# A gated cross-attention and expert layer on one core: result rows in 4 KB pieces, reloads on two queues, a short block moved up, and four sums shared by two engines

## The reference

```
x = x + tanh(g0) * attention(layernorm(x), ctx)      # one head; keys: 64 of ctx and 64 of x per sequence
x = x + tanh(g1) * moe(layernorm(x))
moe(xf):
  probs = softmax(xf @ gate_w.T)                      # 8 experts
  top_p, top_i = top_k(probs, 2)
  y  = sum over the 2 experts of top_p * (silu(xf @ fc1_e.T) * (xf @ fc2_e.T)) @ proj_e.T     # width 176
  y += sigmoid(xf @ shared_gate.T) * (silu(xf @ s1.T) * (xf @ s2.T)) @ shared_proj.T          # width 704
```

## Time and profile before

| | |
|---|---|
| median of 3 executions | 301.57 us (300.46 to 302.14) |
| profiled execution | 300.09 us, span 298.3 us |
| TensorE busy | 276.1 us (93%) |
| VectorE busy | 215.4 us (72%) |
| ScalarE busy | 170.5 us (57%) |
| GpSimd busy | 131.5 us (44%) |
| last chain, largest | TensorE 55%, VectorE 24%, ScalarE 8% |

### The profile page before, as it was taken

How to read it: one execution, slowest core, us unless ns; L and a number is a source line. 1 busy time by engine, 2 the same in 40 slices (tenths; PEclk the granted TensorE clock), 3 DMA queues, 4 the chain that set the end, 5 groups by cost and what they waited for, 6 DMA issues and landing times.

```text
span 298.3 us, 5868 instructions
## 1 busy us (share of the span) xinstructions
PE 276.1 (93%) x1785; PEld 247.7 (83%) x1785; DVE 215.4 (72%) x698; ACT 170.5 (57%) x399; POOL 131.5 (44%) x163
## 2 busy tenths in 40 slices
PE   3987999999998899999999999799999999999991
PEld 3876878789787687798888888699999999998881
DVE  3864876979968858767876767877877787763285
ACT  1666777688557447574235465366676667654230
POOL 3430541451685245445550000057777787775000
PEclk9999999999999999999999999999999999999998
DMA  7470216212027021544324654358888888756796
GB/s 209 167 248 4 73 55 230 70 53 73 20 65 280 21 91 55 192 142 139 129 77 163 218 196 143 103 107 141 130 141 138 137 135 142 117 68 71 258 355 233
DMA packets 30511, 40.18 MB, mean 135 GB/s; under 512 B 2961, under 2 KB 26641, under 8 KB 30481
## 3 DMA queue, kind: packets, MB, share of 16 engines
q1 hardware_dynamic: 22336, 29.53, 31.5%
q0 software_dynamic: 7152, 9.57, 19.4%
q10 hardware_dynamic: 992, 0.71, 0.8%
HBM read 22.68 MB, written 17.11 MB: 133 GB/s over the span
## 4 chain that ended last, share of the span: by engine, by line
PE 55%; DVE 24%; ACT 8%; issue 6%; POOL 3%; DMA 3%; DVEq 0%; SPq 0%; ACTq 0%; POOLq 0%
PE bank L415 42%; PE bank L658 6%; DVE ew_lo L1011 4%; PE bank L753 3%; ACT ew_hi L776 3%; DVE work L1341 3%; PE bank L709 3%; ACT sh_hi L776 2%; DVE neg_max L1055 2%; DVE xt_lo L1011 2%; DVE work L1363 2%; ACT work L808 1%; DMA xn_all<-x_dram 1%; DVE sh_lo L1011 1%; DMA weight_stage<-ew_dram 1%
## 5 line engine op out<-in xcount | busy, mean ns | idle before, releaser
L1533 POOL DMA_INDIRECT y_d<-work,dest_of_slot x39 | 60.5, 1552 | 56.9 <-DVE dest_of_slot L1387 55.3
L415 PE MATMUL bank<-ew_hi,xt_hi 128*128 (+2 forms) x172 | 53.7, 322 | 1.1 <-DVE xt_lo L1011 0.8
L415 PE MATMUL bank<-ew_lo,xt_hi 128*128 (+2 forms) x172 | 51.8, 301 | 0.0
L415 PE MATMUL bank<-ew_hi,xt_lo 128*128 (+1 forms) x133 | 40.5, 305 | 0.0
L1011 DVE TENSOR_TENSOR xt_lo<-bank,xt_hi 128x256 fp32r<-128x256 f32 (+2 forms) x90 | 35.6, 398 | 3.0 <-ACT xt_hi L776 1.5
L1493 POOL DMA_INDIRECT xs_d<-xn_all,slot_of_pair x32 | 32.9, 1029 | 10.1 <-issue 7.3
L415 PE MATMUL bank<-xt_hi,sw_hi 128*128 128x512 f32 x88 | 34.8, 395 | 0.2 <-DVE work L1341 0.2
L776 ACT ACTIVATE xt_hi<-bank 128x256 fp32r<-128x256 f32 (+1 forms) x90 | 32.7, 409 | 3.4 <-PE bank L753 2.2
L415 PE MATMUL bank<-xt_lo,sw_hi 128*128 128x512 f32 x88 | 34.5, 392 | 0.0
L415 PE MATMUL bank<-xt_hi,sw_lo 128*128 128x512 f32 x88 | 34.3, 390 | 0.0
L1011 DVE TENSOR_TENSOR ew_lo<-bank,ew_hi 128x512 fp32r<-128x512 f32 (+1 forms) x41 | 22.7, 581 | 15.9 <-ACT ew_hi L776 15.7
(11 more groups left out here) (159 smaller groups left out, 680.9 us busy)
## 6 DMA issues: line engine op xcount, KB each, us to landing
work<-xs_d SPq DMA_DIRECT2D x39, 136.0 KB, 2.5
weight_stage<-ew_dram SPq DMA_DIRECT2D x10, 486.5 KB, 3.8
ew_hi<-y_d SPq DMA_DIRECT2D x8, 512.0 KB, 7.6
y_d<-work SPq DMA_DIRECT2D x6, 512.0 KB, 3.7
work<-ctx_t_dram SPq DMA_DIRECT2D x4, 512.0 KB, 3.7
xn_all<-x_dram SPq DMA_DIRECT2D x3, 512.0 KB, 6.0
xs_d<-pad_row SPq DMA_DIRECT2D x9, 136.0 KB, 1.8
weight_stage<-sw_dram SPq DMA_DIRECT2D x3, 384.0 KB, 3.4
```

Source lines behind the costliest of these rows:

```text
L415: last = nc.tensor.matmul(dst, a, b, start=(n == 0), stop=(n == len(pairs) - 1))
L1533: nc.gpsimd.indirect_dma_start(out=y2_d, out_offset=bass.IndirectOffsetOnAxis(ap=IX[:, n:n + 1], axis=0), in_=EY[:, n % 4, :], in_offset=None,
```

## The change

There are five edits.

- A token's row in `y2_d` is now `(chunk, p, j)` and no longer `(chunk, j, p)`, so the four rows of a partition are adjacent and one piece of a store or reload is 4 KB where it was 1 KB. `C_TOK` follows.
- The reloads of copy 1 are issued by ScalarE, two behind `s_hi(3,1)` (after its own wait for all scatters) and two behind `s_hi(3,2)`; SP issues those of copy 0.
- In the last chunk TensorE's order becomes `... pj(3,2), fc(3,4), fc(3,5), pj(3,3), pj(3,4), pj(3,5)`.
- Combines 4 and 5 stand between product and low half of blocks 4 and 5, one each; they stood behind the low half of block 4, both. Combines 6 and 7 stay behind the low half of block 5.
- The four sums of chunk 2 are split. VectorE does tile 0 ahead of the expert steps (waiting for that tile alone, `p_pre`) and tile 1 at the end of step 0; ScalarE does tiles 2 and 3 at the end of step 0 (`a_z`). TensorE's steps 1, 2 and 3 wait for the bank that each needs. `v_z` counts two less from there.

```
-        y2_t = y2_d[0:TOP * N_TOK, :].rearrange("(i c j p) d -> i c p j d", i=TOP, c=N_CH, j=TPC)
+        y2_t = y2_d[0:TOP * N_TOK, :].rearrange("(i c p j) d -> i c p j d", i=TOP, c=N_CH, j=TPC)
...
             def store_sums(s):
-                sp.wait_ge(v_z, 4 * s + 4)
+                sp.wait_ge(v_z, 4 * s + 4 if s < PRE - 1 else 4 * s + 2)
+                if s == PRE - 1:
+                    sp.wait_ge(a_z, 2)
...
             for c in LAST_FIRST:
-                for i in range(TOP):
-                    sp.dma_start(Y2[i][:, c * TPC:(c + 1) * TPC, :], y2_t[i, c]).then_inc(d_y[i][c], 16)
+                sp.dma_start(Y2[0][:, c * TPC:(c + 1) * TPC, :], y2_t[0, c]).then_inc(d_y[0][c], 16)
...
+                    if (s, j) == (PRE - 1, S_FULL) and t < TPC - 1:
+                        last.then_inc(p_pre, 1)
...
-                if s == 1:
-                    pe.wait_ge(v_z, 4 * PRE)
+                if s in (1, 2):
+                    pe.wait_ge(v_z, 4 * (PRE - 1) + s)
+                if s in (2, 3):
+                    pe.wait_ge(a_z, s - 1)
...
-            blocks(PRE, N_CH, 1)
+            fc(LAST, 1)
+            for j in range(2, S_BLK):
+                if j < S_FULL:
+                    pj(LAST, j - 2)
+                fc(LAST, j)
+            for j in range(S_FULL - 2, S_BLK):
+                pj(LAST, j)
...
+                if s == 0:
+                    act.wait_ge(d_z, 16 * (PRE - 1))
+                    for t in (2, 3):
+                        T = (PRE - 1) * TPC + t
+                        if t == 2:
+                            act.wait_ge(p_pre, 3)
+                        else:
+                            act.wait_ge(p_pj, 6 * PRE)
+                        copy(SX2[:, t, :], B[4 + t][:, 0:D], scale=GS[:, T:T + 1]).then_inc(a_z, 1)
...
+            for j in range(S_BLK):
+                s_silu(LAST, j)
+                s_hi(LAST, j)
+                if j == 1:
+                    for r in range(4):
+                        act.wait_ge(d_ey[r], 16 * len(range(r, SLOT_TILES, 4)))
+                if j in (1, 2):
+                    for c in LAST_FIRST[2 * j - 2:2 * j]:
+                        act.dma_start(Y2[1][:, c * TPC:(c + 1) * TPC, :], y2_t[1, c]).then_inc(d_y[1][c], 16)
...
+                if s == 0:
+                    dve.wait_ge(p_pre, 2)
+                    s_sum(PRE - 1, 1)
...
-            s_sums(PRE - 1)
+            dve.wait_ge(d_z, 16 * (PRE - 1))
+            dve.wait_ge(p_pre, 1)
+            s_sum(PRE - 1, 0)
             e_steps(e_step)
 
             for j in range(S_BLK):
                 s_mult(LAST, j)
-                if j == 3:
-                    combine(0)
+                if j >= 3:
+                    combine((0, 4, 5)[j - 3])
                 s_lo(LAST, j)
...
-                if j == 4:
-                    combine(4)
-                    combine(5)
-                if j == 5:
-                    combine(6)
-                    combine(7)
-            s_sums(LAST)
+            combine(6)
+            combine(7)
+            for t in range(TPC):
+                s_last(t)
...
-    consts[:, C_TOK:C_DUM] = np.arange(TOP * N_T)[None, :] * P + np.arange(P)[:, None]
+    tile = np.arange(TOP * N_T)
+    consts[:, C_TOK:C_DUM] = (tile // TPC * CH + tile % TPC)[None, :] + np.arange(P)[:, None] * TPC
```

More of the change, by code:

```diff
@@ L227, in build @@
         g_pay, e_ix = map(sem, ("g_payload", "e_ix"))
+        p_pre, a_z = sem("p_pre"), sem("a_z")
         zeroed, tanh_g, rw_hi, rw_lo = map(sem, ("zeroed", "tanh_g", "rw_hi", "rw_lo"))
@@ L401, in _ @@
             for t in range(LAST * TPC + 1, N_T, 2):
-                sp.wait_ge(v_z, t + 1)
+                sp.wait_ge(v_z, t - 1)
                 sp.dma_start(out_t[t], XNR[:, t, :]).then_inc(d_out, 16)
@@ L655, in pj @@
                             pe.wait_ge(v_hl, 6 * s + j + 1)
-                        if j == 0 and n == 0 and s > 0:
+                        if j == 0 and n == 0 and 0 < s < LAST:
                             pe.wait_ge(v_z, 4 * s - 3 + t)
@@ L680, in _, with blocks @@
             pe.wait_ge(sw_lo, SW_PIECES)
-            def blocks(s0, s1, ahead):
-                order = [(s, j) for s in range(s0, s1) for j in range(S_BLK)]
+            def blocks(ahead):
+                order = [(s, j) for s in range(PRE) for j in range(S_BLK)]
                 for n in range(ahead, len(order) + 2):
-                    if n == len(order) and s1 == PRE:
+                    if n == len(order):
                         pe.wait_ge(v_h, 6 * PRE - 1)
@@ L689, in blocks @@
                         xx(1, 1, 16)
-                    if n == len(order) + 1 and s1 == PRE:
+                    if n == len(order) + 1:
                         pe.wait_ge(ew_lo, E_PIECES)
@@ L766, in _ @@
             pj(0, 1)
-            blocks(0, PRE, 4)
+            blocks(4)
             e_steps(e_step)
             pe.wait_ge(e_h, SLOT_TILES)
-            blocks(PRE, N_CH, 1)
+            fc(LAST, 1)
[5 more added lines that the diff above has]
+                pj(LAST, j)
         @block.scalar
@@ L1002, in _ @@
             for t in range(LAST * TPC, N_T, 2):
-                act.wait_ge(v_z, t + 1)
+                act.wait_ge(v_z, t - 1)
                 act.dma_start(out_t[t], XNR[:, t, :]).then_inc(d_out, 16)
@@ L1352, in expert_weights, with s_sum, s_last @@
                     .then_inc(ew_lo, 1)
+            def s_sum(s, t):
+                T = s * TPC + t
+                nc.vector.tensor_scalar(SX2[:, t, :], B[4 + t][:, 0:D], GS[:, T:T + 1], None, ALU.mult).then_inc(v_z, 1)
             def s_sums(s):
[L1355 to L1358, removed]
-                    dve.wait_ge(v_c2, 2)
[L1360 to L1367, removed]
+                dve.wait_ge(p_pj, 6 * s + 6)
+                at_least(dve, d_z, 16 * s)
+                for t in range(TPC):
+                    s_sum(s, t)
+            def s_last(t):
+                T = LAST * TPC + t
+                if t == 0:
+                    dve.wait_ge(v_c2, 2)
+                dve.wait_ge(p_end, t + 1)
+                nc.vector.scalar_tensor_tensor(out=XNR[:, T, :], in0=B[4 + t][:, 0:D], scalar=GS[:, T:T + 1],
+                                               in1=XNR[:, T, :], op0=ALU.mult, op1=ALU.add).then_inc(v_z, 1)
             def e_step(s, u, m):
```

## The result

Twenty executions of each kernel: 299.91 us after (298.49 to 302.04), 301.88 before. The ratio is 0.9933, interval 0.9915 to 0.9950, which is 2.0 us of 301.88. The forecast was 298.8, 2.8 less than before; the measured time lies in its range of 297.7 to 300.4. The direction was right, and 0.8 us of gain didn't come. So the two spans must not be subtracted: the joints are compared by distances inside one trace.

What follows compares the result with a forecast made beforehand. TensorE, busy throughout the expert steps, was taken as the bound, so only that stretch's two ends pay: 300.09 - 1.6 (start) - 1.3 (tail) + 0.1 (stores) = 297.3, plus 1.48 is 298.8 us; range 297.7 to 300.4.

Steps and rivals of the forecast that it cites:

- Start: Entry to the expert steps: splitting chunk 2's sums lets up(3) start earlier; gain taken as 1.6 us, lower bound 0.95.
- The 0.35 "issue" gap: TensorE ahead of up(2): register work behind a blocked queue, 0.35 us, taken as gone; up to two such gaps possible.
- Rival C: Expert-step start pays half: ScalarE's copies and VectorE's sum delay step 1, or register gaps stay; gain 0.6, 299.8; chance 0.11.
- the signs named for the right case: Trace checks, among them TensorE idle under 0.3 us between up(1) and up(2), and up(3) 5.8 us after up(0).
- Tail: Last chunk after fc(3,4): new block order and combine places start the last sums earlier; gain 1.33 us, bounds 0.5 to 1.4.
- T: End of fc(3,4) on TensorE, 286.72 us in the profile before; the forecast's tail times count from it.
- the landing of the third pair: Chunk 1's reloads: landed at 287.3 in the old profile; margin ahead of combine 4 of 0.7 us, 1.6 at 396 GB/s.
- rival B: Tail: a combine waits for its reload, holding up VectorE and pj(3,4); 2.0 us late gives 300.1; chance 0.11.
- Second queue: Reloads: engines are full with one queue at a DMA share of 1.09, so a second was priced at nothing.
- the 0.1 for the stores: Last stores at the kernel's end: 0.1 us added to the sum for the last 1.57 MB going out.
- rival D: Expert steps: scatters slow down with the new row order; landing 7.5 us costs 6.7 us, 306; chance 0.05.
- rival E: Both joints: no effect at all, since they wait for something the trace puts elsewhere; 301.5; chance 0.06.

Runs made afterwards that it cites:

- the register experiment: Changed kernel with up(3)'s registers and addresses made ready in step 2 ahead of pj(0)'s wait, and up(3) issued ahead of pj(1)'s address work; ratio 0.9909.
- combines early: Changed kernel with each combine moved one place earlier in the last chunk, 5 beside block 4, 6 beside block 5, 7 last; ratio 0.9929.

## Why the prediction was right, and where it missed

**Start.** Forecast 1.6, measured 1.02 (8.43 to 7.41). The mechanism was right in every step that was named: the sum alone takes 0.48 (0.47 forecast), the product is through in time for the transposes behind up(1), ScalarE's two copies delay its silu by 0.03 only (3.46 after up(0), 3.43 before), and pj(0) doesn't wait. The term that was mis-sized is "The 0.35 "issue" gap ... I take it as gone". It moved from up(2) to up(3) and grew to 0.41, and restarting a chain cost another 0.23 (1.20 for six matmuls instead of 0.97): 0.64, which the register experiment gave back as 0.65. The lower bound, 0.95, covered it. The measured 1.02 was shown to be this edit's own by the kernel with the sums only (1.04); since the old start varies from 8.43 to 8.83 and the new one from 7.33 to 7.56, one pair of traces fixes it to a few tenths only. Rival C, "the start pays half", came true in part: its second cause, the register gaps, held, its first didn't, and the gain lies between its 0.6 and the forecast's 1.6. Of the signs named for the right case, all that the traces show came but one: up(3) starts 6.37 us after up(0), not 5.8 (it is 5.8 with the registers ahead).

**Tail.** Forecast 1.33, measured 1.20. The order of the blocks works as written: pj(3,3) and pj(3,4) fill the time, and combines 4 and 5 hide beside ScalarE's high halves. The missing 0.13 is small slips in the steps of block 5: its product was put at T plus 2.68, inside the low half that ends at 2.73, and starts 2.77 after TensorE's 289.01. What the forecast left on the path are combines 6 and 7 ahead of the last sums: one of them moved up gave 0.58 (6.17 to 5.59).

**Reloads.** Here a step failed that the total doesn't show. The text says of the bigger pieces "Neither enters the sum, since no combine waits for a reload now". They enter it with 0.9 to 1.2 us: with pieces of 1 KB the changed kernel has a tail of 7.38, and the tail alone on the kernel before gains 0.32. The error was in the landing of the third pair, put at three quarters of the bytes, 11.0 us after the first issue. With 1 KB it was there 13.2 to 13.4 us after it, in the three traces where combine 4 waited for it. With 4 KB it was 10.3 to 10.7, in the three where it waited (288.20 less 277.73 with combines early). By then the queues had moved 3.9 to 4.1 MB with 1 KB (307 GB/s over 13.16 us, for one) and 3.6 to 3.7 MB with 4 KB (347 over 10.47), of 4.19 in all, and not three quarters: many loads are under way at once, and a pair isn't finished when its share of the bytes has passed. So the margin was not 0.7 but less than nothing, and rival B was the rule for small pieces; the rise from about 360 to 420 GB/s, larger than the 396 that the rows gave, turned it. The forecast came out right because the change holds both edits, which is in part luck: a pair that takes 10.3 to 10.7 us from 278.43 leaves combine 4, at 290.27, a margin of 1.1 to 1.5 (an estimate from these traces, near the forecast's 1.6), but without the bigger pieces there is none. The Trainium skill, page "DMA: Bandwidth & Descriptors", section "Why small descriptors are slow (HBM only)", gives a fixed cost for each packet; its direction agrees with these traces, while the estimate of 6% made from it is less than half of the 16% measured (421 against 361). (The forecast's 0.9 us for it is 6% of 13.7; its 1.2 is taken from 11.8, of which 6% is 0.75.)

**Second queue.** Priced at nothing, and that held for the change: 360 GB/s with two queues, tail 6.17 with one. The issues on ScalarE took 0.85 and 0.81 a pair, in the places given for them. The 0.28 that it cost with 1 KB pieces in the old order is one trace's, and its cause is open.

**Rest.** The middle is 90.72 in most traces and 90.85 in three; that 0.13 comes and goes without a change of code. From the last sums to the end of the span it is 4.18 before and 4.19 after, so the 0.1 for the stores wasn't needed. The scatters' landing, 3.9 with the new rows alone, didn't change (rival D), nor was the change without effect (rival E). The sum by distances: 1.02 plus 1.20 less 0.13 is 2.09, against 2.0 by the timed runs.

## What to carry to other kernels

When a stall goes, look at what the sequencer does right behind it: address work that a wait held back stays on the path until it is issued ahead of that wait. The landing of a load in a full queue isn't its share of the bytes; measure it, and if an edit moves a reader forward, test it without the edit that speeds the loads. An edit that is worth nothing alone (4 KB rows, 0.9992) can carry most of another's gain. And where a chain's last piece is TensorE's, look whether the engine that is released was free before it.

## What the runs showed of the hardware

The code before up(0) took from 187.60 to 191.27 us in the fourteen traces (only the pieces of a few hidden stores differ in it), with mean granted clocks of the whole span from 0.997 down to 0.980. In the changed kernel's trace the clock fell in two places where it stayed at 1.00 before (stretches, columns of the earlier trace rows):

```profile
18.00:24.00 6.00, 3.84 (x21) 3.64 (x20) 2.33 (x6) 3.94 (x10) 0.17 (x1) 0.72 0.76 270
100.00:110.00 10.00, 8.59 (x51) 7.07 (x49) 5.70 (x20) 4.22 (x13) 5.41 (x9) 0.83 0.23 84
```

The first lies behind an idle time of TensorE of 2.16 us (1.24 at that place before), as its timeline shows:

```profile
20.56 0.58 PE L417 MATMUL bank<-ew_hi 128*128 128x256 f32 x1 [2.16 <-DVE ew_lo L1037]
20.93 0.42 PE L417 MATMUL bank<-ew_lo,ew_hi 128*128 128x256 f32 x1
21.15 0.41 PE L417 MATMUL bank<-ew_hi,ew_lo 128*128 128x256 f32 x1
```

There matmuls start 0.21 apart until 23.7, where the granted clock is 0.50, the level of 1.2 GHz, and 0.12 apart at 2.4 GHz after it. With the changed code the trace of the kernel with all sums on VectorE reached up(0) at 188.03 and a clock of 0.997, so the change alone doesn't cause it. What does is open. Single executions of the changed kernel differ by 3.5 us (298.49 at a mean clock of 1.000, 302.04 at 0.984), more than the whole effect that was studied; how much of that the clock makes isn't shown.
